# Layer-0 attention: the bulk loads on ScalarE's queue, a head's maxima transposed one step later, the maximum products last in a step

## The reference, cut to what matters

```python
q, k, v = (proj(Wq), proj(Wk), proj(Wv))          # 2 x 16 heads x 1024 x 32
q = q * cos + rotate_half(q) * sin
k = k * cos + rotate_half(k) * sin
scores = jnp.einsum('bhqd,bhkd->bhqk', q, k) / math.sqrt(HD)
scores = jnp.where(causal, -jnp.inf, scores)
attn = jax.nn.softmax(scores, axis=-1)
out = jnp.einsum('bhqk,bhkd->bhqd', attn, v)
```

## Time and profile before

| | us |
|---|---|
| median of 3 runs | 3534.2 |
| profiled execution, device time | 3544.96 |
| its span in the trace | 3543.2 |
| TensorE busy in the span | 2902.2 (82%) |
| ScalarE busy | 1183.5 (33%) |
| queue q1, share of 16 DMA engines | 19.6% |

### The profile page before, as it was taken

One profiled execution on the slowest core, in us unless ns is written; L12 is line 12 of the kernel. 1 busy time (PEld: TensorE's weight loads), 2 busy tenths in 40 slices (PEclk: granted clock), 3 DMA queues, 4 the chain that ended last, 5 costly groups with the idle time before them and its releaser, 6 DMA issues. The chain is left out here.

```text
span 3543.2 us, 42139 instructions
## 1 busy us (share of the span) xinstructions
PE 2902.2 (82%) x14636; PEld 2309.4 (65%) x14636; DVE 1942.3 (55%) x3582; ACT 1183.5 (33%) x2287; POOL 943.5 (27%) x664
## 2 busy tenths in 40 slices
PE   7928777677899999446799999678999995388994
PEld 6815455455688888335688888566888883267773
DVE  5626566558223322435466666665666666667755
ACT  2205444453211111113244444333444442233331
POOL 1205565564111111302200000131000001266643
PEclk9958888898899999778899999889999996699997
DMA  4652223312200000374000000121000002210002
GB/s 175 234 182 66 88 91 95 90 40 95 72 18 19 18 18 1 113 275 171 26 21 31 31 21 31 57 96 36 21 31 31 21 27 95 72 36 26 10 1 95
DMA packets 120190, 236.93 MB, mean 67 GB/s; under 512 B 9632, under 2 KB 63904, under 8 KB 119296
## 3 DMA queue, kind: packets, MB, share of 16 engines
q1 hardware_dynamic: 120064, 235.30, 19.6%
HBM read 162.14 MB, written 72.88 MB: 66 GB/s over the span
## 5 line engine op out<-in xcount | busy, mean ns | idle before, releaser
L1059 POOL TENSOR_TENSOR l0a_probs_hl<-l0a_probs,l0a_probs_hl 128x896 fp32r<-128x896 f32 (+1 forms) x128 | 285.3, 2241 | 278.6 <-ACT l0a_probs L987 278.5
L1291 PE MATMUL l1a_obank<-l1a_pT_hl,l1k_v_hl 128*128 128x512 f32 (+3 forms) x1152 | 300.8, 370 | 7.2 <-DVE l1a_pT_hl L1364 7.1
L1364 DVE TENSOR_TENSOR l1a_pT_hl<-l1a_work,l1a_pT_hl 128x512 fp32r<-128x512 f32 (+3 forms) x384 | 212.9, 555 | 155.8 <-ACT l1a_pT_hl L1324 155.6
L1317 ACT ACTIVATE l1a_probs<-l1a_scores,l1a_row 128x128 f32<-128x128 f32 (+7 forms) x256 | 189.6, 742 | 318.1 <-DVE l1a_row L1354 318.1
L1271 PE MATMUL l1a_scores<-l1k_kT_hl,l1a_qa_hl 128*128 128x512 f32 (+3 forms) x1152 | 291.8, 362 | 1.5 <-ACT l1a_probs L1317 1.5
L1407 POOL TENSOR_TENSOR l1a_q_stage<-l1k_qpe,l1a_ones 128x512 fp32r<-128x512 f32 x32 | 33.3, 1041 | 877.2 <-PE l1a_work L1299 820.2
L1009 DVE TENSOR_REDUCE l0a_halves<-l0a_mbank 128x1 f32<-128x512 f32 (+3 forms) x256 | 139.4, 586 | 173.6 <-PE l0a_mbank L930 170.9
L986 ACT ACTIVATE l0a_probs_hl<-l0a_sbank 128x896 fp32r<-128x896 f32 (+1 forms) x128 | 124.4, 972 | 303.3 <-PE l0a_sbank L952 181.0
L1299 PE MATMUL l1a_work<-l1a_wov,l1a_oT_hl 128*128 128x512 f32 x768 | 216.7, 405 | 5.0 <-DVE l1a_oT_hl L1383 3.0
L1696 DVE TENSOR_TENSOR f0f_hid<-f0f_silu,f0f_ubank 128x512 f32<-128x512 f32 x64 | 44.0, 687 | 321.5 <-PE f0f_ubank L1631 321.5
L1324 ACT CAST l1a_pT_hl<-l1a_work 128x512 fp32r<-128x512 f32 (+3 forms) x384 | 183.7, 478 | 108.5 <-PE l1a_work L1282 107.3
(11 more groups left out here) (258 smaller groups left out, 6334.3 us busy)
## 6 DMA issues: line engine op xcount, KB each, us to landing
v_dram<-l0f_v_rows SPq DMA_DIRECT2D x24, 768.0 KB, 4.5
qk_dram<-l0f_stage SPq DMA_DIRECT2D x8, 2048.0 KB, 11.0
l1a_wov<-wov_dram SPq DMA_DIRECT2D x32, 512.0 KB, 3.3
l0a_v_stage<-v_dram SPq DMA_DIRECT2D x8, 1536.0 KB, 15.5
l1a_wabs<-wabs_dram SPq DMA_DIRECT2D x32, 384.0 KB, 3.9
l0a_q_stack<-qk_dram SPq DMA_DIRECT2D x32, 256.0 KB
l0a_k_stack<-qk_dram SPq DMA_DIRECT2D x32, 256.0 KB
wov_dram<-w1a_wov SPq DMA_DIRECT2D x16, 512.0 KB, 3.3
```

What stands on the lines that cost most here:

```text
L1059: nc.gpsimd.tensor_tensor(probs_hl[:, r, 1, 0:wide], probs[:, r, 0:wide], f32(probs_hl[:, r, 0, 0:wide]), ALU.subtract).then_inc(low_done, 1)
L1291: last = pe.matmul(obank[:, c:SPAN], src["v_hl"][:, a, n, :], pT_hl[:, ring(n, s), b, c:SPAN], start=(n == 0 and i == 0), stop=(n == QT * ...
L1317: nc.scalar.activation(probs[s][:, first:first + wide, :].rearrange("p k c -> p (k c)"), scores[:, n % S_AHEAD, 0:wide * P], ACT.Exp, bias ...
L1364: nc.vector.tensor_tensor(pT_hl[:, r, 1, c:SPAN], work[:, slot, c:SPAN], f32(pT_hl[:, r, 0, c:SPAN]), ALU.subtract).then_inc(work_free[slo ...
```

## The change

Three things. `load_stack` and `load_values` are issued from ScalarE's queue: the prologue ahead of ScalarE's first exponential, with stack 2 now ahead of the values of group 0; stack h+4 behind the exponential of the last unit (u == 5) of head h; the values of group g+1 (g from 1) behind the exponential of unit 24g + 7, the second unit of a head. SyncE keeps the maximum copies and the traffic of the sums. N goes from k == 0 to k == 1, so that it is three steps ahead of Z0. The two M of a step go behind its L, P and O.

The diff, without the bodies of `load_stack` and `load_values`, which move from `@block.sync` to `@block.scalar` with `act` in the place of `sp`:

```diff
         h, k = divmod(i, U)
-        if k == 0 and 0 <= h + 1 < HEADS:
+        if k == 1 and 0 <= h + 1 < HEADS:
             yield "N", i, h + 1
         if 0 <= i + 2 < HEADS * U:
             yield "Z", i, i + 2
-        if h + 2 < HEADS:
-            yield "M", i, 2 * (h * U + 2 * U + k)
-            yield "M", i, 2 * (h * U + 2 * U + k) + 1
         if 0 <= i < HEADS * U:
             yield "L", i, i
...
             yield "O", i, 2 * (o // U) + (o % U == U - 1)
+        if h + 2 < HEADS:
+            yield "M", i, 2 * (h * U + 2 * U + k)
+            yield "M", i, 2 * (h * U + 2 * U + k) + 1
...
         @block.sync
-            load_stack(0)
-            load_stack(1)
-            load_values(0)
-            load_stack(2)
-            load_stack(3)
-            load_values(1)
-            sp.dma_start(*next_load).then_inc(next_loaded, 16)
...
-                if k == 4 and 0 <= h and h + STACKS < HEADS:
-                    load_stack(h + STACKS)
-                if k == LAG + 2 and h >= 1 and (h - 1) % GROUP_HEADS == GROUP_HEADS - 1 and (h - 1) // GROUP_HEADS + 2 < GROUPS:
-                    load_values((h - 1) // GROUP_HEADS + 2)
...
         @block.scalar
+            load_stack(0)
+            load_stack(1)
+            load_stack(2)
+            load_values(0)
+            load_stack(3)
+            load_values(1)
+            act.dma_start(*next_load).then_inc(next_loaded, 16)
             for kind, i, n in steps_layer0():
...
                     nc.scalar.activation(probs[:, r, 0:wide], sbank[:, n % 2, 0:wide], ACT.Exp).then_inc(exp_done, 1)
+                    h, u = divmod(n, U)
+                    if u == U - 1 and h + STACKS < HEADS:
+                        load_stack(h + STACKS)
+                    group, rest = divmod(n - LAG - 4, U * GROUP_HEADS)
+                    if rest == 0 and 1 <= group and group + 1 < GROUPS:
+                        load_values(group + 1)
+            act.wait_ge(next_loaded, 16)
```

More of the change, by code:

```diff
@@ L830, in _ @@
         def _(sp):
[L831 to L849, removed]
             def store_sums(h):
@@ L914, in _ @@
                 load_inverse(group)
-            sp.wait_ge(next_loaded, 16)
         @block.tensor
@@ L978, in _, with load_stack, load_values @@
         def _(act):
+            def load_stack(h):
+                b, g, j = h // NH, h % NH // GROUP_HEADS, h % GROUP_HEADS
+                slot, rows = h % STACKS, slice(j * HD0, (j + 1) * HD0)
+                if h >= STACKS:
+                    act.wait_ge(scores_full, (h - STACKS + 1) * U)
+                act.dma_start(f32(q_stack[0:2 * HD0, slot, :]), qk_dram[b, 0, :, g, rows, :]).then_inc(stack_loaded[slot], 16)
+                act.dma_start(f32(q_stack[2 * HD0:QW, slot, :]), qk_dram[b, 0, 0, g, rows, :]).then_inc(stack_loaded[slot], 16)
+                act.dma_start(f32(k_stack[0:HD0, slot, :]), qk_dram[b, 1, 0, g, rows, :]).then_inc(stack_loaded[slot], 16)
+                act.dma_start(f32(k_stack[HD0:QW, slot, :]), qk_dram[b, 1, :, g, rows, :]).then_inc(stack_loaded[slot], 16)
+            def load_values(group):
+                b, g = divmod(group, KT)
+                slot = group % 2
+                if group >= 2:
+                    act.wait_ge(values_done, (group - 1) * GROUP_HEADS * U)
+                act.dma_start(f32(v_stage[:, slot].rearrange("p t j c -> p t (j c)")),
+                             v_dram[b, g].rearrange("t p c -> p t c")).then_inc(v_loaded[slot], 16)
+                act.dma_start(v32_stage[:, slot].rearrange("p t j c -> p t (j c)"),
+                             v32_dram[b, g].rearrange("t p c -> p t c")).then_inc(v_loaded[slot], 16)
+            load_stack(0)
[5 more added lines that the diff above has]
+            act.dma_start(*next_load).then_inc(next_loaded, 16)
             for kind, i, n in steps_layer0():
```

## The result

| | before | after |
|---|---|---|
| median of the runs, us | 3538.64 (3527.57 to 3544.41, 4 runs) | 3478.10 (3474.41 to 3479.80, 4 runs) |
| profiled execution, us | 3544.96 | 3474.41 |
| 29 heads, from maximum copies to maximum copies | 475.7 | 425.6 |
| plain head | 13.4 | 12.7 |
| group of four heads (mean of five, from one issue of values to the next) | 67.6 | 60.1 |

What follows compares the result with a forecast made beforehand. Waits, mainly for maximum copies behind stack loads, bound the attention, with no engine full. 29 x 12.4 + 50 = 410 us instead of 475.7 gains 66, with the start 78: 3456 us from 3534.2, range 3435 to 3485 (8 in 10: 3412 to 3512).

Steps and rivals of the forecast that it cites:

- Part 1: Maximum copies get their own queue: landing 3 to 4 us from N, no single losses (87 us) in the 29-head loop.
- all 87 us of single losses: Loop of 29 heads: 475.7 us less 29 x 13.41 (389), lost in single places, one per group of four heads.
- the tail: A stack load's rows on very few DMA engines, lasting until the next stack, with parts of small copies in line behind.
- the copies still stand behind the tail: Slower rival, N to Z0: stays 8.45 us, a head 15.9 us, total about 3590 us; chance 0.08.
- Part 2: Loads on ScalarE: stack issues cost nothing; values block 10 us, pausing 6.4 plus 2 us cold clock, six places, 50 us.
- Part 3: N one step later, M last: new N wait 0.6 to 0.7 us, net gain 1.0 us a head, 29 us in all.
- Part 4: Start: copies go out near 235, first exponentials near 261; gain 13 us at most, 12 taken.
- The sum: Whole stage: 29 heads go from 475.7 to 410 us, gain 66; with the start 78, forecast 3456 us.
- The two queues share what generates their DMAs: Rival, SyncE's copies blocked during ScalarE's issues: covered in steady state, start's gain may be gone, 3468 us; chance 0.15.
- The few engines with the tail are the bound: Rival, plain head: 13.2 us a stack whatever the queue, gain 0.2 not 1.0 us, 23 us more, 3479; chance 0.14.
- The stack's issues uncovered: Rival, ScalarE: a stack's issues not covered, 62 us more, 3518 us, no measurable change; chance 0.07.
- the short block: Rival, values' issue on ScalarE: only 1.1 to 5 us, no pause, 50 us less, 3406 us; chance 0.06.

Runs made afterwards that it cites:

- The cut kernel: The changed kernel with each 64-row load of a stack cut into two loads of 32 rows, still on ScalarE's queue: 3395.24 us, ratio 0.9580.
- the two cut kernels on SyncE: The kernel before with 64-row stack loads cut into 32-row loads, all loads on SyncE: 3421.77 us in the old order, 3388.36 us in the new order.

## Why the prediction was right, and where it was off

**Direction and mechanism: right.** The copies left the stack's line, and with them the six waits of 7.6 to 9.6 us went; the split's went with the order. The kernel with the loads alone shows the queue's 40.5 us, the difference of the two the order's 21.2.

**Part 1, "all 87 us of single losses go, and in the plain head nothing but TensorE's own work and the pauses around N is left": this step failed in size.** The plain head was to be 12.4 us and is 12.7, 29 x 0.3 = 9 us. The cut kernel, with 12.4 and no wait for copies, shows the cause: the tail still holds two of the eight parts of each copy, though they have a queue of their own. In the packet records of the plain head above the last parts of the copy that was issued at 293.87 go 2.6 us after the others. I had weighed "the copies still stand behind the tail" against "a landing soon after", 3 to 4 us from N; it was 6.1 us. And I had set that against three mean steps, 6.2 us, while the three steps in question are short ones: the cut kernel does them in 5.4 us (287.45 to 292.82). So copies that I would have called just in time are late by 0.2 to 0.6. The Trainium skill, DMA: Bandwidth & Descriptors, section "Queues, rings and completion order", which I had cited for it, says that an engine turns from one queue's ring to the next after a whole packet of several descriptors. That is a wait behind part of the line, not a free pass, and I had read the rule for its sign and not for its size. The trace doesn't bear the rule out as it stands. At 0.155 us a row, 2.6 us are 17 rows; but once a part of the copy has gone (297.78) the engine takes a single row before the 4 bytes that signal this part (297.96), and the late parts of the second copy of the pair, issued 0.68 us behind the first, go 0.65 us behind those of the first, after four rows and not another 17. So the engine turned after single rows here, and yet each copy of this pair was held back about 2.6 us. What holds it stays open.

**Part 2, the stack's issues at nothing: right.** They take 2.1 us on ScalarE and no wait of TensorE in a plain head is on ScalarE (the last heads have two, of 0.2 and 0.3 us). **The values at 10 us with a pause of 6.4 and 2 us of cold clock: the block mis-sized, a second pause left out.** The block is 7.8 to 8.5 us in four of the six places and 0.6 and 0.9 in two. The four show a first wait for ScalarE of 3.8 to 4.5 us, and the two one of 2.1 for the copies instead: 3.4 on average for my 6.4. But each place has a second wait in the next head, for copies that share the engines with the values, 1.6 to 3.2 us, 2.4 on average. Behind each of the six first waits, and behind the three second ones of 2.8 to 3.2 us, the 4 us that follow have a granted clock of 0.50 to 0.58; behind the three second ones of 1.6 to 2.0 it is 0.70 to 1.00. In all 425.6 - 29 x 12.7 = 57.3 us in six places, 9.6 each, for my 8.4: 7 us more. So two errors of opposite sign partly cancel in this term. What the 3.7 us beside the two waits are wasn't taken apart; the low clock is one part. I did see the length of the issue as the line of the stack ahead of it ("I expect less line ahead"), and then took the engine's own 10 us all the same; four kernels put it at 0.4 to 0.9 at the median where the line is cut, has cleared or is in another queue.

**Part 3: right.** N's new wait was to be 0.6 to 0.7 us and is 0.61; the net gain was to be 1.0 us a head, and is 1.0 (13.7 to 12.7) between the kernel with the loads alone and the after, and 1.0 (13.4 to 12.4) between the two cut kernels on SyncE. What I had not seen is that it is worth nothing without part 1, and that the new wait needn't be there: shortened by one reduction it is worth 13 us by the last copies, with the tail cut 22.

**Part 4: right in mechanism, 2 us too high.** First exponentials were to be near 261 and start at 261.69; the copies were to go out near 235 and do at 234.82. Unit 2 follows at 263.47, and the second copies are 9.9 us earlier for my 12.

**The sum.** Of the predicted 78 us, 9 are missing by the plain head, 7 by the values' places and 2 by the start. That leaves 60, and the medians give 60.5. The profiled executions differ by 70.6; 61.7 of that lie ahead of the last copies. The other 8.9 were not taken apart; the profiled execution of before was 6.3 us over its median and that of after 3.7 under.

**The rivals.** *The copies still stand behind the tail* is refuted: N to Z0 is 6.1 us and not 8.45. *The two queues share what generates their DMAs* had the start's gain at nothing; SyncE issued its copies in 0.82 us at 234.82, inside ScalarE's issue of 16.43 (223.19 to 239.62). The Trainium skill, Perfetto Trace Analysis, section "DMA Instruction — HWDGE (DVE, Sync)", has the generator locked for one DMA at a time; this row shows no such lock between these two engines while the one stands in a long issue. *The few engines with the tail are the bound*, at 3479, names the measured time to a microsecond, and that is luck: I had the plain head at 13.2 and nothing else lost, and it is 12.7, with the rest lost in the values' places and the start. But its cause, the two engines, is behind most of what my forecast missed, and behind far more than I gave it: 83 us in the kernel after, 120 in the kernel before. I had the row that told it, named its reading, and priced it at 23 us, since I asked what the tail would cost the change and not what it cost. *The stack's issues uncovered* and *the short block* did not occur.

## What to carry to other kernels

A DMA share that stays at one tenth between bursts was here a load on two of 16 engines: look at the outer dimension of its access pattern before you move it to another queue, for the cut of two lines was worth more than the whole rearrangement, which with the cut is worth only its order. A long issue of a DMA came here only with a line ahead of it in its own queue (though not each time), so look at the DMA before it. And two waits of one loop must be priced as a pair: the order gained nothing alone, 21 us with the other queue and 28 with the cut.

## What the runs showed of the hardware that was not expected

- A load written as a [2, 32, 1024] piece ran on two engines at 52 GB/s; cut into loads of 32 rows a stack went in bursts of 200 to 300 GB/s.
- The second issue of values took 8.0 (ScalarE) and 10.8 us (SyncE) at the median behind uncut stacks on the same queue, though 0.6 and 0.9 in two of ScalarE's six places, and 0.39 (nine units later), 0.58 (on the other queue) or 0.88 us (stacks cut) without.
- A copy of 4 KB on a queue of its own was held back 2.6 us at an engine that another queue kept busy with 4 KB rows, though the engine took single rows in turn with the copy's own parts.
- Two engines' queues accepted DMAs at once, one of them in the middle of the other's issue of 16.4 us.
